# One mixture-of-experts kernel: pieces loaded ahead of x, sums and turns moved, scales and weights placed earlier

## The reference

```python
# per batch entry; side is (1024, 1), cond is (1, 1024), x is (1024, 1024)
adj = side * cond * softmax(x) / sqrt(1024);  adj[diagonal] = -inf
mask = 1.0 at the 10240 largest of the 1024 * 1024 elements of adj, else 0.0
# the mask goes through an 8-expert layer
scores = softmax(mask @ G);  value, index = top_k(scores, 2);  w = value at index, else 0
gated = silu(mask @ gate_w[e].T) * (mask @ up_w[e].T)
out = sum_e w[e] * gated @ down_w[e].T
out = out + sum_e w[e] * (mask @ lora_A[e].T) @ lora_B[e].T
result = x + out
```

## Time and profile before

| | |
|---|---|
| median of 3 runs | 862.33 us (860.84 to 862.92) |
| the profiled execution | 862.85 us |
| its span, first to last instruction | 861.1 us |
| granted TensorE clock, mean of the span | 0.822 of full speed |
| TensorE busy | 534.7 us (62%) |
| VectorE busy | 521.0 us (61%) |
| ScalarE busy | 454.5 us (53%) |
| GpSimd busy | 390.8 us (45%) |
| moved by DMA | 159.93 MB, mean 186 GB/s |

### The profile page before, as it was taken

One profiled execution on the slowest core, in us unless ns is written; L12 is line 12 of the kernel. 1 busy time (PEld: TensorE's weight loads), 2 busy tenths in 40 slices (PEclk: granted clock), 3 DMA queues, 4 the chain that ended last, 5 costly groups with the idle time before them and its releaser, 6 DMA issues.

```text
span 861.1 us, 14614 instructions
## 1 busy us (share of the span) xinstructions
PE 534.7 (62%) x4178; PEld 365.4 (42%) x4178; DVE 521.0 (61%) x1242; ACT 454.5 (53%) x655; POOL 390.8 (45%) x337
## 2 busy tenths in 40 slices
PE   0311484378877945788869327868869249689810
PEld 0200463355544624555546114544546136456500
DVE  6768699486577675666876266566853335224335
ACT  6685488567643773566437154684536226455410
POOL 7132200233373116675872224775851347757610
PEclk9755598599898986789989767898989659999965
DMA  9970430224132833575368424684558237866659
GB/s 318 360 201 0 174 121 25 61 79 140 55 126 80 322 124 118 185 256 198 127 233 326 174 89 154 224 274 140 180 197 334 87 125 271 266 220 223 241 218 382
DMA packets 80443, 159.93 MB, mean 186 GB/s; under 512 B 22889, under 2 KB 32105, under 8 KB 79856
## 3 DMA queue, kind: packets, MB, share of 16 engines
q1 hardware_dynamic: 59760, 108.60, 36.6%
q0 software_dynamic: 20608, 50.37, 17.0%
HBM read 107.53 MB, written 73.40 MB: 210 GB/s over the span
## 4 chain that ended last, share of the span: by engine, by line
PE 23%; DVE 18%; DMA 16%; issue 14%; ACT 11%; POOL 9%; DVEq 4%; SPq 3%; POOLq 1%; ACTq 0%
PE pa L676 8%; ACT mask L791 7%; DMA out_dram<-piece 6%; DMA piece<-put_rows 3%; DMA xg<-mask_rows,where 3%; DVE mask L1060 3%; PE pb L663 2%; DMA put_rows<-y,where 2%; DVE w L1166 2%; PE pc L699 2%; PE pc L702 2%; PE pc L700 2%; PE pc L701 2%; ACT y L848 2%; DMA w<-put_rows 2%
## 5 line engine op out<-in xcount | busy, mean ns | idle before, releaser
L676 PE MATMUL pa<-w,xt 128*128 x1472 | 211.1, 300 | 5.7 <-issue 4.8
L676 PEld LDWEIGHTS pa<-w,xt 128*128 128x128 f16 x1472 | 152.3, 104 | 66.5 <-issue 16.9
L848 ACT ACTIVATE y<-pc,where 128x512 f32<-128x512 f32 x184 | 123.9, 687 | 90.4 <-PE pc L702 52.5
L517 POOL DMA_INDIRECT put_rows<-y,where x92 | 92.7, 1007 | 153.0 <-ACT y L848 130.9
L1336 DVE SCALAR_TENSOR_TENSOR g_full<-pa,where,s_act 128x144 f32<-128x144 f32 x92 | 33.6, 365 | 208.7 <-ACT s_act L840 190.2
L509 POOL DMA_INDIRECT xg<-mask_rows,where x92 | 98.9, 1074 | 119.2 <-DVEq L1328 89.6
L835 ACT ACTIVATE xt<-pb 128x1024 f16<-128x1024 f16 x92 | 94.3, 1025 | 93.7 <-PE pb L663 86.7
L840 ACT ACTIVATE s_act<-pa,small 128x128 f32<-128x128 f32 x92 | 33.8, 367 | 135.6 <-PE pa L676 134.4
L663 PE MATMUL pb<-ident,xg 128*128 128x128 f16 x736 | 62.7, 234 | 56.8 <-DMA xg<-mask_rows,where 35.5
L699 PE MATMUL pc<-wd,gt 128*128 x184 | 76.3, 415 | 27.4 <-ACT y L848 27.1
L526 POOL TENSOR_TENSOR piece<-piece 128x512 f32<-128x512 f32 x48 | 61.3, 1277 | 57.4 <-DMA piece<-put_rows 55.5
(11 more groups left out here) (208 smaller groups left out, 874.2 us busy)
## 6 DMA issues: line engine op xcount, KB each, us to landing
piece<-put_rows SPq DMA_DIRECT2D x96, 256.0 KB
v<-in_x_dram SPq DMA_DIRECT2D x40, 512.0 KB, 8.9
piece<-in_x_dram SPq DMA_DIRECT2D x48, 256.0 KB
out_dram<-piece SPq DMA_DIRECT2D x48, 256.0 KB
mask_rows<-mask SPq DMA_DIRECT2D x4, 2048.0 KB, 16.7
w<-put_rows SPq DMA_DIRECT2D x16, 512.0 KB, 9.7
w<-in_L_ffn_gate_w_dram SPq DMA_DIRECT2D x8, 512.0 KB, 10.2
w<-in_L_ffn_up_w_dram SPq DMA_DIRECT2D x8, 512.0 KB, 8.3
```

Of the source, the lines that this page charges most:

```text
L517: pool.indirect_dma_start(out=put_rows[n % 2], out_offset=bass.IndirectOffsetOnAxis(ap=put_row[n][:, i:i + 1], axis=0), in_=y[:, g % NY, : ...
L676: last = pe.matmul(l1[g % 2], xt[:, g % 2, t, :], w1[:, bass.ds(e, 1), t, k, :].rearrange("p o n -> p (o n)"), start=(t == 0 and k == 0), ...
L848: nc.scalar.activation(y[:, g % NY, half * HALF:(half + 1) * HALF], pc[:, half, :], ACT.Copy, scale=y_scale[n][:, i:i + 1]).then_inc(y_rea ...
```

## The change

Nothing is computed differently; instructions change their places in their queues.

- *Pieces.* `PIECE_AT` has pieces 9 to 15 summed at tiles 13 to 19, not 14 to 20. With `PIECES_FIRST` 14, `move_mask` stands in SyncE's queue behind the load of piece 15, the last, not of piece 14.
- *Sums of counts.* TensorE sums count 1 at (5, 0), not (4, 3); count 2 at (7, 2), not (7, 1); count 3 at (10, 0), not (9, 2). The aims that read counts 2 and 3 move to (8, 0) and (10, 1), and ScalarE's four parts of count 3 move one spot back each.
- *Mask sum, check, turns.* The sum of the mask moves from (17, 3) to (18, 1), the check from (18, 1) to (18, 2). The eight turns and their copies now stand in the same spots 0 and 2 of tiles 19 to 22; the turns began at (18, 3) before and were at spots 1 and 3, the copies at (18, 2) and then at spots 0 and 2.
- *Weights.* In `route`, `weigh` comes ahead of `place_pairs`, and a drain is gone.
- *Scales.* In the prologue `largest_norms` comes ahead of the first half of the mask, and `make_scales` between the halves.

```diff
@@ the tables @@
-    AIM_AT = {(2, 2): 1, (5, 1): 2, (7, 2): 3, (10, 0): 4}
+    AIM_AT = {(2, 2): 1, (5, 1): 2, (8, 0): 3, (10, 1): 4}
...
-                    (6, 0): (2, 1), (6, 1): (2, 2), (6, 2): (2, 3), (8, 0): (3, 0), (8, 1): (3, 1),
-                    (8, 2): (3, 2), (9, 0): (3, 3)}
-    SUM_AT = {(4, 3): 1, (7, 1): 2, (9, 2): 3}
+                    (6, 0): (2, 1), (6, 1): (2, 2), (6, 2): (2, 3), (8, 1): (3, 0), (8, 2): (3, 1),
+                    (9, 0): (3, 2), (9, 1): (3, 3)}
+    SUM_AT = {(5, 0): 1, (7, 2): 2, (10, 0): 3}
...
-    MASK_SUM_AT = (17, 3)
-    CHECK_AT = (18, 1)
-    TURN_AT = {(18, 3): 0, (19, 1): 1, (19, 3): 2, (20, 1): 3, (20, 3): 4, (21, 1): 5, (21, 3): 6, (22, 1): 7}
-    STORE_MT_AT = {(18, 2): 0, (19, 0): 1, (19, 2): 2, (20, 0): 3, (20, 2): 4, (21, 0): 5, (21, 2): 6, (22, 0): 7}
+    MASK_SUM_AT = (18, 1)
+    CHECK_AT = (18, 2)
+    TURN_AT = {(19, 0): 0, (19, 2): 1, (20, 0): 2, (20, 2): 3, (21, 0): 4, (21, 2): 5, (22, 0): 6, (22, 2): 7}
+    STORE_MT_AT = dict(TURN_AT)
...
-    PIECE_AT = {**{j + 1: j for j in range(9)}, **{j + 5: j for j in range(9, PIECES)}}
-    PIECES_FIRST = 13
+    PIECE_AT = {**{j + 1: j for j in range(9)}, **{j + 4: j for j in range(9, PIECES)}}
+    PIECES_FIRST = 14
@@ route @@
                 choose(n)
+                weigh(n)
                 place_pairs(n)
-                weigh(n)
-                dve.drain()
                 fill_table(n)
                 take_slots(n)
@@ the prologue on VectorE @@
+            largest_norms()
             make_mask(0, range(0, 4))
-            largest_norms()
+            make_scales()
             make_mask(0, range(4, C))
-            make_scales()
             check_mask(0)
```

## The result

| | before | after |
|---|---|---|
| median of 3 runs each | 862.33 us (860.84 to 862.92) | 834.15 us (831.84 to 836.23) |
| ratio, 95% interval | | 0.968 (0.963 to 0.972) |
| the profiled execution, its span | 862.85, 861.1 | 836.23, 834.5 |
| granted clock, mean of the span | 0.822 | 0.838 |

The kernel is 28 us faster, and the profiled executions lie 26.6 us apart. The next table splits the gain by stage. A batch begins where VectorE takes the slots (L1318); its row sum is that of the next mask (L1064), `choose` begins at L1217. The forecast's terms stand beside it, put to the stage in which each was to show.

What follows compares the result with a forecast made beforehand. Waits between queues, not one line, were taken to bound the kernel, the largest hole in batch 1 after the mask stretch. Terms summed to -37.1, plus 3 for low clock: -34, from 862.85 to 829 us, range 813 to 850.

Steps and rivals of the forecast that it cites:

- Pieces: Batches 1 and 2: earlier sums and piece 15 loaded before the mask wait remove the waits of 14.2 and 10.94 us: -25.1.
- puts beside x: Rival: the two y buffers wait for puts of 9 us or more, half of 25.1 returns, 841 us; chance 0.12.
- reordering does nothing: Rival: piece 15 lands with the mask because its packets mix with x's, all 25.1 stay, 854 us; chance 0.05.
- slower: Rival: SyncE reaches move_mask late behind piece 13's store, the stall returns, x and mask come late, 867 us; chance 0.04.
- Turns: Tiles 19 to 22: second turns and the last score wait for copies, 7.8 us in each of three batches: +24.4.
- turns hide better: Rival: half of the turns' 24 us is hidden, needing ScalarE's copies done sooner, 817 us; chance 0.14.
- the clock falls at every turn wait: Rival: twelve low-clock second layers of 1.7 us, 20 us instead of 3, giving 846 us; chance 0.13.
- Mask sum: Behind tile 18's first layer: that layer and the turn of x fill the wait, about 3 us of it stay: -12.4.
- Sums further back: Count sums on TensorE moved later so layers fill their waits; 6.1, 5.4 and 7.0 us in three batches: -18.5.
- Last batch: Piece 15 summed at tile 19, not 20, so the chain put, y, put ends about 2.7 us earlier: -2.7.
- Weights before places: VectorE's weights fill most of the wait for ranked, one drain fewer; -0.5 in the prologue, -0.4 per batch: -1.7.
- Scales: Prologue: the first expert's cut and B's leave ScalarE before the transposes need it: -1.1.

Runs made afterwards that it cites:

- queue order alone: Kernel before with PIECES_FIRST = 14 and nothing else, the load of piece 15 ahead of x on SyncE: 837.8 us, ratio 0.973.
- piece edit alone: Kernel before with sums of pieces 9 to 15 one tile earlier and the mask's move behind piece 15's load: 840.5 us, ratio 0.973.
- old turns: Kernel after with turns and their copies back at their old spots, mask sum and check at the new ones: 817.7 us, ratio 0.947.
- weights alone: Kernel before with the pairs' weights ahead of their places and one drain fewer: 866.5 us, ratio 1.001.
- old places: Kernel after with turns and copies put back and places computed ahead of weights again: 818.5 us, ratio 0.952.
- short adds: Kernel after with turns and copies put back, both GpSimd adds of a piece cut to 8 of 512 columns: 810.6 us, ratio 0.941.

## Why the prediction was right, and where its terms were not

The forecast was 829 us with a range of 813 to 850; the kernel takes 834. It named the parts that gain and the part that costs, and both were there.

*Pieces: right.* -25.1 forecast; 14.2 and 10.9 us are gone from the profile to the tenth (17.84 and 14.58 down to 3.66), and in medians the edit alone brought 22.8. The mechanism as told, a load that stands behind x and the mask because its buffer's store does, is shown by the run with the queue order alone. The long working on when sums 9 to 13 would run was not needed for it (sum 13 began at 443.5 in the piece edit alone, not 447.3), and its 4.1 us for a store was a mean of waits with the two stalls of 16 us in it; the other 33 give 3.4. The rivals *puts beside x*, *reordering does nothing* and *slower* are all out: ScalarE waited 6.8 us for puts, piece 15 landed in time, and in the kernel after 3.8 us lie between the store that was said to decide and the load that waits for it, against 4 assumed and 16 needed.

*Turns: right, in mechanism and nearly in size.* 2.0, 2.0, 0.9, 0.9 and 2.0 us a batch were forecast from the two copies of the earlier trace rows; the trace has 1.95, 1.95, 0.84, 0.84 and 1.70. Put back, they gave 8.9, 7.0 and 8.0 us a batch, 24 in all, against 24.4 forecast and 3 for a lower clock beside it. Both are in the 24: the waits are 21.8, and TensorE's busy time in the three stretches is 2.0, -0.1 and 1.8 us above that with the old turns. The tests named ahead hold: second turns wait about 2 us at tiles 19 and 20, and the stretch from the mask's sum (267.52) to `choose` (303.13) is 35.6 us, 5.2 over the 30.4 before. The rivals *turns hide better* and *the clock falls at every turn wait* are out. Among the turns the clock did fall, once in each batch: in batch 0 behind the first wait of 1.95 us (matmuls of 0.63 us at 277.91, a first layer of 2.80) and not behind the equal wait a tile later (0.38 at 286.27), in batch 1 behind the first too, in batch 2 behind the second.

*Mask sum: right.* -12.4 forecast; 12.0 by the two runs that differ in it and its check alone. The wait in the kernel after is 3.46, 0.25 and 2.13 us, where 3 was taken.

*Sums further back: the term that was mis-sized.* -18.5 forecast, -12 measured: 3.7, 3.8 and 4.5 us where 6.1, 5.4 and 7.0 were taken. The waits of TensorE at L571 in batches 1 and 2, 7 us a batch, were counted right. The step that failed there is the one that priced what comes next: "it can't run ahead by all of it: I take 5.4 and 7.0". It allowed 2.6 and 1 us of the 8 for GpSimd's queue, and nothing for the gathers' own time. Once TensorE ran ahead, 7 us more of waits for gathers came in each of these batches. The gathers stand in GpSimd's queue behind pieces that wait for their DMAs, and beside the pieces they take 5.1 us to land, not 3.5. That the adds do not set them is shown; how the two others share them is an estimate. In batch 0 the term lost 2.4 us to ScalarE's late counts, whose cause is open; without them the profiles have the 6.1 us (7.2 and 5.7). The moves of counts 2 and 3, priced at 4.2 together in each batch, brought 4 us in all three beyond what count 1's had brought, in single profiles.

*Last batch: wrong, small.* -2.7 forecast, 0 measured: 166.2 us in the piece edit alone, 165.6 in the mean of the six profiles with the pieces moved and the adds whole, 165.3 in that of the six with neither. The chain put, y, put was read from one put issued 4.3 us behind its y; two puts later GpSimd had already waited 3.69 us for y in the kernel before, so the late put had slack behind it. The price was taken at the wrong end of that slack; this is read from the trace, and no run tried it.

*Weights before places: right in sign, mis-sized.* -0.5 in the prologue and -0.4 a batch forecast; -0.8, and -0.9, -0.7 and -0.5 in the kernel after, held against the kernels without the stall (17.25 us in the prologue; 17.75, 17.3 and 17.7 from `choose` to the slots): the wait for `ranked` goes and so do the drain and the gap. It holds only while the probabilities are in time; at 817.7 us they are not, which was the term's bound of 0.

*Scales: right.* -1.1 forecast. The prologue is 2.0 us shorter with the weights' 0.8 in it; against the mean of the seven profiles with neither edit (157.6) the kernel with the new scales and the old places (156.8) gives -0.8, and the mean of the five with both edits (155.67) against the one with the weights alone (157.23) gives -1.6.

Together the terms as measured (-25.1, -12, -12, +24, -2.9, -0.8, 0) make -29; the profiled executions lie 26.6 apart and the medians 28.2.

## What to carry to other kernels

Ask of each load in a shared DMA queue what stands ahead of it that it does not need: here one load behind 6 MB cost 11 to 14 us in each of two batches, and one integer took it away. When a wait is taken from one engine, price the next queue from its own waits: an engine that already waits for DMAs a little can give back much of what is gained. Price a DMA by what it takes beside the others that will be in flight: a gather of 3.5 us took 5.1 beside the pieces. And two uses of one buffer want the longest available work between them: spreading the turns one behind each layer, as before, beats putting them in pairs by 16 us, so half of a mixed change can be worth more than the whole.

## What the runs showed of the hardware

A gather of 128 rows takes longer to land beside other transfers of the same core. From the start of its issue to its landing it took 3.3 to 3.8 us in batch 0 of the kernel after (tiles 6 to 13) and 3.4 to 8.1 us in batch 1 (tiles 7 to 13), where SyncE moves pieces of 256 KB at the same time; the issue on GpSimd took 1.0 us in both, so the difference lies behind it. What the two kinds of transfer share there no run shows.

An instruction of VectorE with two inputs in SBUF runs long while GpSimd does a tensor operation, and this sums up. In batch 1 of the kernel before, L1344 takes 778 ns in the mean and 458 with GpSimd's adds cut; over the whole profile it takes 0.31 us at each of the 51 places where no tensor operation of GpSimd lies over it, and 0.90 in the mean at the 41 where one does. L951 falls from 1406 to 1279 ns. L1336 and L1338, which read PSUM, and L1004, with one large input, stay within 1%. Of VectorE's 88.66 us 9.0 went with the adds (these two lines are 7 of them), and 6.4 and 5.6 us of the length of the stretch in batches 1 and 2; between the two kernels with the old turns it was 4.8 and 3.1. The kernel after has its largest case, L1014 in 4.00 us beside one operation of 2.14 us, where its shortest takes 1.27:

```profile
406.44 4.00 DVE L1014 SCALAR_TENSOR_TENSOR mask<-v,small 128x1024 f32<-128x1024 f32 x1
...
407.21 2.14 POOL L479 TENSOR_TENSOR t_row<-v,mask 128x1024 f32<-128x1024 f32 x1
```

The Trainium skill (SBUF — State Buffer, "Who interferes with whom") says that VectorE and GpSimd share one port pair under an exclusive lock, and that a VectorE instruction with two SBUF inputs contends for it with a GpSimd instruction that reads SBUF. By it, the two-input lines suffer and the others don't, and these traces agree, line by line. The Trainium skill has, in the same section, the order of issue decide who is held up. By that GpSimd would wait in the case shown, as VectorE's start is the earlier one by 0.77 us; the rows show VectorE long instead, if GpSimd's start in the profile can be trusted.

The clock of TensorE after short waits is not settled by their length. Matmuls ran at the lower of its two levels (0.63 us, 1.2 GHz) after waits of 4.09 and 2.04 us. Of the six waits of 1.95 us in the kernel after, three were followed by it and three by matmuls at the upper level (0.38 us, 2.4 GHz); and after a wait of 1.77 us at count 2's sum of batch 0 the kernel after ran at the upper level and the one with short adds, from the second matmul on, at the lower.
